# Dividing the spread-field loads between two DMA queues by tiles instead of by partition halves

## The reference

```python
e = jnp.stack([tbl_f[ids[:, f]] for f in range(39)], axis=1)     # (2048, 39, 16)
x0 = xk = e
for idx, (W, b) in enumerate(params):                            # 3 layers, 128 outputs each
    z = jax.nn.relu(jnp.einsum('bhd,bkd,hks->bsd', x0, xk, W) + b[None, :, None])
    if idx != 2:
        xk = z[:, :64, :]
        direct.append(z[:, 64:, :])
    else:
        direct.append(z)
z = jnp.sum(jnp.concatenate(direct, axis=1), axis=-1)
h = jnp.concatenate([z, dense_ctx], axis=1)
h = jnp.maximum(h @ W_top1 + b_top1, 0.0)
h = jnp.maximum(h @ W_top2 + b_top2, 0.0)
y = h @ W_top3
```

## Time and profile before

| | |
|---|---|
| median of 3 runs | 2412.33 us (2410.93 to 2412.48) |
| profiled execution, its own time | 2410.21 us |
| its span | 2408.4 us |
| busy: TensorE, VectorE, GpSimd, ScalarE | 97%, 94%, 83%, 54% |
| chain that ended last | TensorE 95%, line 718 alone 92% |
| mean DMA rate | 197 GB/s |

### The profile page before, as it was taken

The page is one execution under the profiler, slowest core; times in us unless marked ns, Lnnn a source line. Parts: engine busy times, 40 slices in busy tenths (PEclk is TensorE's granted clock), DMA queues, the critical chain, the costliest instruction groups (busy, mean ns, idle before and its releaser), DMA issues.

```text
span 2408.4 us, 32379 instructions
## 1 busy us (share of the span) xinstructions
PE 2343.9 (97%) x7936; PEld 1499.0 (62%) x7936; DVE 2253.5 (94%) x2241; ACT 1305.4 (54%) x1534; POOL 2001.8 (83%) x1284
## 2 busy tenths in 40 slices
PE   2899999999999999999999999999999999999999
PEld 1566666666666666666666666666666666666655
DVE  3799999999999999999999999999999999999973
ACT  2455555555555555555555555555555555555542
POOL 5888898898888889889888888988888888898630
PEclk9999999999999999999999999999999999999999
DMA  7977887787787788778778778877877887887610
GB/s 196 229 189 201 220 214 186 211 232 179 207 229 199 193 217 213 187 211 235 178 207 226 199 194 217 225 179 211 231 182 203 226 204 191 214 225 182 197 57 1
DMA packets 403715, 475.43 MB, mean 197 GB/s; under 512 B 171409, under 2 KB 180625, under 8 KB 403425
## 3 DMA queue, kind: packets, MB, share of 16 engines
q1 hardware_dynamic: 304055, 310.13, 52.8%
q10 hardware_dynamic: 79163, 159.95, 21.6%
q0 software_dynamic: 20480, 5.15, 1.8%
HBM read 465.41 MB, written 9.71 MB: 197 GB/s over the span
## 4 chain that ended last, share of the span: by engine, by line
PE 95%; POOL 2%; DMA 2%; issue 1%; SPq 0%; ACT 0%; DVE 0%; ACTq 0%; POOLq 0%
PE z L718 92%; POOL rows L515 1%; DMA xb<-x_rows 1%; POOL low L546 1%; DMA rows<-table,index 0%; PE x L813 0%; PE z L832 0%; PE prod_dve L813 0%; PE z L834 0%; PE z L791 0%; PE z L837 0%; SPq L426 0%; DMA x_rows<-rows 0%; PE x L814 0%; PE x L815 0%
## 5 line engine op out<-in xcount | busy, mean ns | idle before, releaser
L546 POOL TENSOR_TENSOR low<-prod_pool,high 128x1024 fp32r<-128x1024 f32 (+1 forms) x576 | 1379.4, 2395 | 206.8 <-ACT high L886 200.1
L718 PE MATMUL z<-prod_whole,w_whole 128*128 128x512 f32 (+2 forms) x2432 | 1130.5, 594 | 42.2 <-DVE prod_whole L601 42.2
L718 PE MATMUL z<-high,w_high 128*128 128x512 f32 (+1 forms) x1792 | 864.4, 482 | 17.9 <-ACT high L886 13.7
L886 ACT ACTIVATE high<-prod_pool 128x1024 fp32r<-128x1024 f32 (+1 forms) x576 | 611.0, 1061 | 407.5 <-DVE prod_pool L601 234.5
L718 PEld LDWEIGHTS z<-prod_whole,w_whole 128*128 128x128 f32 (+2 forms) x2432 | 461.8, 190 | 426.9 <-issue 365.6
L718 PE MATMUL z<-high,w_low 128*128 128x512 f32 (+1 forms) x1792 | 708.4, 395 | 0.0
L515 POOL DMA_INDIRECT rows<-table,index x640 | 611.1, 955 | 116.0 <-issue 102.2
L601 DVE TENSOR_TENSOR prod_pool<-xh,x 128x1024 f32<-128x1024 f32 x512 | 622.8, 1216 | 36.4 <-ACT x L864 33.3
L601 DVE TENSOR_TENSOR prod_whole<-xh,x 128x1024 f32<-128x1024 f32 (+1 forms) x576 | 615.6, 1096 | 6.1
L886 ACT ACTIVATE high<-prod_dve 128x1024 fp32r<-128x1024 f32 (+2 forms) x384 | 338.8, 882 | 481.6 <-DVE prod_dve L601 319.3
L718 PE MATMUL z<-low,w_high 128*128 128x512 f32 (+1 forms) x1664 | 554.4, 427 | 0.6 <-POOL low L546 0.6
(11 more groups left out here) (59 smaller groups left out, 405.2 us busy)
## 6 DMA issues: line engine op xcount, KB each, us to landing
xh<-x_rows SPq DMA_DIRECT2D x63, 2560.0 KB, 17.7
xh<-x_rows ACTq DMA_DIRECT2D x63, 2432.0 KB, 19.2
xb<-x_rows SPq DMA_DIRECT2D x128, 546.0 KB
xb<-x_rows SPq DMA_DIRECT2D x63, 468.0 KB
xa<-x_rows SPq DMA_DIRECT2D x191, 78.0 KB
rows<-table,index POOLq DMA_INDIRECT x640
xh<-x_rows SPq DMA_DIRECT2D x65, 128.0 KB, 20.5
x_rows<-rows SPq DMA_DIRECT2D x256, 20.0 KB
```

The costliest lines, as they stand in the source:

```text
L546: pool.tensor_tensor(low[0:g.rows, g.split_slot, 0:n, :], prod_pool[0:g.rows, g.slot, 0:n, :], high[0:g.rows, g.split_slot, 0:n, :].bitcas ...
L718: return pe.matmul(z[stage][:, :], weights[0:g.rows, table[stage, g.tiles[i]], :], src[0:g.rows, i, :], start=g.begins_layer and first, st ...
L886: act.activation(high[0:g.rows, g.split_slot, 0:n, :], src[0:g.rows, 0:n, :], ACT.Copy).then_inc(high_ready, 1)
```

## The change

Each queue takes both partition halves of its tiles. SyncE loads tiles 0 to 8 (SECOND = 9), in two DMAs of 64x9x512; ScalarE loads tiles 9 to 18, in two DMAs of 64x10x512, and the lone field, in two of 64x512. Within a queue the lower half (part 0) is issued first. The semaphore values that VectorE waits for follow the number of DMAs: six for a buffer instead of three. At the start SyncE's queue issues both halves of tiles 0 to 8 ahead of chunk 1's stores and nothing behind them; ScalarE's issues the lone field's two DMAs and then tiles 9 to 18.

```diff
-SECOND = TK // 2
+SECOND = 9
...
+        def load_tiles(engine, c, loaded, first, end):
+            for part in range(2):
+                load_fields(engine, c, part, loaded, first, end)
+
+        def load_lone_field(engine, c, loaded):
+            for part in range(2):
+                load_fields(engine, c, part, loaded, HALF_TILE, TK, F - 1)
...
                 if c.known and c.n == 0:
-                    for part in range(2):
-                        load_fields(sp, c, part, first_fields_loaded, HALF_TILE, TK, F - 1)
-                    load_first_fields(sp, 0)
+                    load_tiles(sp, c, first_fields_loaded, 0, SECOND)
 
                     store_rows(c + 1)
-                    load_second_fields(sp, 0)
                 else:
-                    load_fields(sp, c, 0, xh_loaded[c.p], 0, TK)
-
-                    load_fields(sp, c, 1, xh_loaded[c.p], HALF_TILE, TK, F - 1)
+                    load_tiles(sp, c, xh_loaded[c.p], 0, SECOND)
...
-                    dve.wait_ge(xh_loaded[c.p], 24 * (c.n - c.p) + 48 * c.p)
+                    dve.wait_ge(xh_loaded[c.p], 48 * (c.n - c.p) + 96 * c.p)
...
-            def load_odd_fields(c):
+            def load_late_fields(c):
...
-                load_fields(act, c, 1, xh_loaded[c.p], 0, HALF_TILE)
+                load_tiles(act, c, xh_loaded[c.p], SECOND, HALF_TILE)
+                load_lone_field(act, c, xh_loaded[c.p])
...
             load_pairs(act, Chunk(0, 0), range(2, JT))
-            load_first_fields(act, 1)
-            load_second_fields(act, 1)
+            load_lone_field(act, Chunk(0, 0), first_fields_loaded)
+            load_tiles(act, Chunk(0, 0), second_fields_loaded, SECOND, HALF_TILE)
```

More of the change, by code:

```diff
@@ L377, in load_fields @@
             engine.dma_start(xh[c.p][part * H:(part + 1) * H, first:end, :], spread).then_inc(loaded, 16)
[L379 to L384, removed]
         def load_pairs(engine, c, shifts):
@@ L915, in chunk @@
                 if begun:
-                    during1[1] = lambda: load_odd_fields(c + 1)
+                    during1[1] = lambda: load_late_fields(c + 1)
                 elif not final:
-                    load_odd_fields(c + 1)
+                    load_late_fields(c + 1)
                 if not begun:
```

## The result

The changed kernel takes 2849.05 us, the median of four runs (2846.08 to 2852.72); the kernel before, run beside it, 2411.63 us (2410.14 to 2412.48). The ratio is 1.182, with an interval of 1.1804 to 1.1836: 437 us slower, where 123 were predicted. The profiled execution took 2852.72 us, its span is 2850.9.

A forecast was written before the change was run, and what follows sets the result against it. TensorE was taken to set the pace, with VectorE close behind and becoming the limit after the change. Border issues 119 us plus start 4 gave 123 on 2410.2, 2533, or 2535.5 as the runs' median; range 2500 to 2620.

The forecast's parts named there:

- The sign and the place: Slower, chance 0.95, at the border between chunks, where ScalarE issues four DMAs instead of one ahead of rounding HALF_TILE.
- three more issues, none waiting: At 62 chunk borders, ScalarE's extra issues delay VectorE by 1.92 us a chunk net, 119 us in all.
- start: In chunk 0, chunk 1's pair loads are issued near 63 and land near 78 us, costing 4 us (-3 to +10).
- rival (a): At each border, ScalarE's queue pushes back on its third or fourth issue: 1.5 us each, 93 more, 2628 us; chance 0.12.
- The last issue ends 0.86 + 0.86 + 0.63 = 2.35 us later: At each border, ScalarE's rounding of HALF_TILE and VectorE's low part start 2.35 us later.
- The argument against (a): SyncE's steady-state pair puts 1344 rows behind unfinished loads without waiting; ScalarE's four put 1408 on an empty queue.
- The 0.43 us a chunk that catch the delay: VectorE's wait for ScalarE's ReLU ahead of stage 2, 0.43 us a chunk, absorbs that much of the 2.35.
- Cost: 0, covered by 8 to 10 us: Steady-state transfers land near 1223 instead of 1217.5 us, but are wanted only at the next border, 1231.4: 0 us.
- Rival (b): Steady-state field loads clash on one half throughout and DMA becomes the bound: 285 us, 2700 us; chance 0.08.
- The halves: Field transfers: one queue on one half moved 212 GB/s, two on opposite halves 398; each half limits at some 200.
- Rival (c): At the borders, extra issues cost under 0.14 us each, VectorE's idle time takes them: not slower, 2412 us; chance 0.05.
- The clock: TensorE's clock in the steady stretch expected at 1.00; below that, it would add time that no term holds.

The follow-up runs named there:

- run 1: Kernel before, with ScalarE's one load of 19 upper tiles cut into four DMAs, halves as before: 2519.85 us, ratio 1.0456.
- run 3: Changed kernel, with the lone field's two small DMAs issued by ScalarE ahead of the two big ones: 2543.87 us, ratio 1.0556.
- run 8: Kernel before, with only the start (order and tiles of chunk 0's loads) taken from the changed kernel: 2421.66 us.
- run 4: Changed kernel, with the lone field's two small DMAs on SyncE's queue in the steady state: 2675.27 us, ratio 1.1101.
- run 5: Kernel before, with the lone field's upper half moved from SyncE to ScalarE, behind its 1216 rows: 2579.31 us.
- run 7: Changed kernel, with ScalarE's four issues behind the second rounding of stage 1 instead of ahead of the first: 2616.63 us.
- run 6: Changed kernel, with SyncE's two field loads held back until VectorE's last product of stage 1: 2763.01 us.
- run 14: Kernel before, with ScalarE's upper half in two DMAs of 16 and 3 tiles: 2417.01 us.
- run 10: Kernel before, with steady-state loads divided by tiles as in the change, lone field first, ScalarE's issues behind the second rounding: 2657.20 us, ratio 1.1033.
- run 13: Kernel before, with ScalarE's upper half in four DMAs issued behind the second rounding, divided by halves: 2409.92 us, ratio 1.000.
- run 2: Kernel before, queues' halves exchanged: ScalarE issues the lower half of 20 tiles, then the lone field's upper half: 2706.68 us, ratio 1.1231.

## Why the prediction was wrong

The sign and the place were right, the mechanism lacked its largest part: issues that wait. The time lies far above the range, which ended at 2620. Runs 1, 3 and 8 divide the 438.7 us between the change (2849.05) and before (2410.31, beside runs 1 and 3):

| term | predicted | measured | from |
|---|---|---|---|
| three more issues, none waiting | 119 | 109.5 | run 1 |
| start | 4 | 10 | run 8 |
| issues that wait for rows ahead | 0 (rival (a): 93) | 305.2 | the change less run 3 |
| run 3's two long chunks, waits for pair loads | 0 | 14 | run 3 less run 1 less 10 |

- **"The last issue ends 0.86 + 0.86 + 0.63 = 2.35 us later"** is the step that failed. Without waiting it holds: run 1 shows 3.19 us for the four and VectorE waiting 2.47. In the change the third and fourth wait as well, and VectorE's wait is 7.34. The argument against (a) failed: it set SyncE's 1344 rows beside ScalarE's 1408 on "an empty queue", as if one queue's ease held for the other. On ScalarE's queue 1024 rows ahead go unhindered at every border and 1216 at none. Why SyncE's second issue, with 1280 ahead, took 0.68 us stays open. It is not that its queue was flowing, for in run 4 an issue of SyncE's waits 11.4 us while its queue moves, and the earlier trace rows had SyncE's pair of 16.2 us. What ends a wait stays open too: in runs 5 and 7 it ends at most borders before ScalarE's queue moves its first packet, in run 6 some 3.5 us after. And the size: (a) was priced at 1.5 us where the wait is about 5. The trace of before gave a hint of that order, which the prediction didn't use, the late beginning of ScalarE's queue: 1201 to 1202 us is the first window after the issue at 1196.28 in which it moves anything.

```profile
q10 hardware_dynamic: 9, 0.02, 5.2%
```

It is a hint only, since the wait isn't measured by that beginning.
- **The 0.43 us a chunk that catch the delay** are too few. Run 1's pace is 37.17, so 2.47 - (37.17 - 35.38) = 0.68 was absorbed; run 14 gives 35.3/45 - 7.3/62 = 0.67. The earlier trace rows had the better figure: VectorE idle for 2000 - 1957.48 = 42.5 us in 56.5 chunks, 0.75 each, of which the earlier trace rows lists only the longest kind. The 10 us between 119 and 109.5 are two errors that partly cancel: the wait is 0.12 us longer than predicted (+7 us in 62 chunks), and 0.25 us more of it is absorbed (-16).
- **"Cost: 0, covered by 8 to 10 us"** for the transfers: right for this kernel, since its chunk is 7 us longer, and wrong as reasoning. The first deadline isn't the next border's fields but SyncE's stores and pair loads behind the fields. With the issues out of the way (runs 10 and 13) the division by tiles costs 247 us. Rival (b) was close to this with 285, but by luck: it had the DMA engines bound all the time, where the runs show loads that come late behind others in one queue. So (b)'s cost stood behind (a)'s, unseen in the profile of the change.
- **The halves.** The reading of the earlier trace rows held: 212 against 398 GB/s then, 265 against 401 in run 10. The Trainium skill says that two concurrent DMAs on the two halves gain only 6% over one ("SBUF — State Buffer", "Can I just issue two DMAs to hit both halves?"). By that the halves would make no difference between runs 10 and 13; the measurement decides against it. The Trainium skill's rule of the port swizzle (same page, "Door 1: The DMA port swizzle"), 8 of the 16 ports for partitions 0 to 63, agrees with these rates.
- **The start.** 4 predicted, 10 in time. Issue at 63 was nearly right (65), the landing at 78 was not (90). The prediction gave the first half of the pairs the engines alone; in the change ScalarE's queue moves 2.27 MB from 70 to 90 us, SyncE's 1.67.
- **Rival (c)**, an issue cheaper than 0.14 us, fell: run 14's issues take 0.69 us (median). **The clock** fell below 1.00, as the text had left open, but VectorE's waits carry the pace without it.
- **Not settled:** what ends an issue's wait, why SyncE's issue at the border goes through, and why the share of the DMA engines is 0.90 in run 13 where it is 0.80 before, at 207 and 208 GB/s.

## What to carry to other kernels

Price a DMA issue on a compute engine by the rows that lie ahead of it in its queue, not by the usual duration of an issue: put small DMAs ahead of big ones, and all of them where that engine isn't waited for. Take an engine's slack from its whole idle time. When transfers get longer, look for the first load behind them in the same queue; its deadline comes before that of the transfer itself.

## What the runs showed of the hardware that was not expected

- An issue on ScalarE's queue at a border took 0.6 to 0.9 us with up to 1024 rows of 2 KB ahead of it (runs 1 and 14; up to 1.1 in run 3), 2.1 to 4.8 with 1216 (run 5), 3.9 to 6.7 with 1280 (run 2) and 3.5 to 6.1 with 1280 in the change, whether two or four DMAs were issued.
- The wait is not one for the queue to begin: it ended before the queue's first packet at most borders of runs 5 and 7 and 3.5 us after it (median) in run 6, and SyncE's issue of run 4 waited 11.4 us while its queue moved 586 packets.
- With SyncE's fields issued at the same time, ScalarE's queue moved its first packets 4.6 to 5.8 us after the issue (before, 62 borders), without them 1.4 to 3.1 (run 6). Two queues that are issued together don't begin together.
- Two queues that each write both halves in turn moved 265 GB/s, two that keep to one half each 401, at a share of 1.05 to 1.07 both times.
